# Local attention's scores in pairs of 32-row products, with one query mask for each batch

## What is computed

```
q, k, v = h @ wq_loc + bq_loc, h @ wk_loc + bk_loc, h @ wv_loc + bv_loc   # 16 heads of 8 features
for each query i, head h:                      # window: keys i-32 .. i+32
    s[j]  = q[i,h] . k[j,h] / sqrt(8) + rel_bias[j - i + 64]
    p     = softmax over the keys j of the window inside the sequence
    out   = sum_j p[j] v[j,h]
```

## Time and profile before

| what | value |
|---|---|
| time, median of 3 runs | 2551.7 us (2546.4 to 2554.1) |
| time of the profiled execution | 2552.2 us |
| its span, first to last instruction | 2550.4 us |
| TensorE busy | 2287.9 us, 90% |
| VectorE, ScalarE, GpSimd busy | 62%, 55%, 37% |
| mean granted clock | 0.959 |
| one loop body (seven of them) | 304.2 to 307.6 us |
| body "first" ends, body "second" begins | 225.7, 2372.9 us |

### The profile page before, as it was taken

How to read it: one execution, slowest core, us unless ns; L and a number is a source line. 1 busy time by engine, 2 the same in 40 slices (tenths; PEclk the granted TensorE clock), 3 DMA queues, 4 the chain that set the end, 5 groups by cost and what they waited for, 6 DMA issues and landing times. The chain is left out here.

```text
span 2550.4 us, 44510 instructions
## 1 busy us (share of the span) xinstructions
PE 2287.9 (90%) x16136; PEld 1618.0 (63%) x16136; DVE 1576.4 (62%) x4246; ACT 1398.1 (55%) x3824; POOL 946.1 (37%) x1058
## 2 busy tenths in 40 slices
PE   7668998989989899999999899898998989989897
PEld 5455666856668466675667656676666756658465
DVE  4555676566665666757666576656676566765752
ACT  4335563755547555566555565465563655647542
POOL 2333551245521544216433165132561235521540
PEclk9878999999999999999999999999999999999999
DMA  4000001000010000100001100000001000010001
GB/s 139 1 1 26 1 2 34 18 31 1 1 42 10 31 1 1 50 15 17 1 6 46 31 1 1 26 26 31 1 1 34 18 31 1 1 42 10 30 1 46
DMA packets 24877, 51.33 MB, mean 20 GB/s; under 512 B 3316, under 2 KB 3900, under 8 KB 24252
## 3 DMA queue, kind: packets, MB, share of 16 engines
q1 hardware_dynamic: 24636, 48.15, 5.8%
HBM read 46.04 MB, written 2.10 MB: 19 GB/s over the span
## 5 line engine op out<-in xcount | busy, mean ns | idle before, releaser
L857 POOL TENSOR_TENSOR rstd<-ve,half_neg 128x4 f32<-128x4 f32 (+1 forms) x56 | 66.4, 1190 | 861.8 <-DVE ve L840 861.8
L1313 PEld LDWEIGHTS ps<-wbuf,QK 128*128 128x128 f32 x2048 | 264.9, 192 | 107.5 <-issue 101.6
L1109 POOL TENSOR_TENSOR E<-E,ri 128x512 f32<-128x512 f32 x240 | 247.4, 1039 | 204.6 <-DVE ri L910 203.3
L1413 ACT ACTIVATE QK<-ps,cols 128x512 f32<-128x512 f32 x256 | 173.5, 686 | 215.1 <-PE ps L1292 214.5
L1292 PE MATMUL ps<-h2T,wbuf 128*128 128x512 f32 x512 | 279.3, 634 | 0.2
L1539 POOL TENSOR_TENSOR work<-work,ri 128x128 f32<-128x128 f32 x480 | 230.8, 505 | 128.4 <-DVE ri L1462 126.6
L748 ACT ACTIVATE E<-ps,nm 128x256 f32<-128x256 f32 x480 | 225.4, 485 | 85.2 <-DVE nm L903 84.4
L1313 PE MATMUL ps<-wbuf,QK 128*128 128x128 f32 x2048 | 267.9, 275 | 0.0
L1532 POOL TENSOR_TENSOR rn<-ss,half_neg 128x8 f32<-128x8 f32 x120 | 195.6, 1637 | 154.2 <-DVE ss L1438 153.5
L1376 ACT ACTIVATE work<-ps,nm 128x128 f32<-128x128 f32 x480 | 198.3, 426 | 81.0 <-DVE nm L1453 77.8
L903 DVE TENSOR_REDUCE nm<-ps 128x2 f32<-128x512 f32 x256 | 169.1, 683 | 98.0 <-PE ps L510 96.9
(11 more groups left out here) (278 smaller groups left out, 4806.3 us busy)
## 6 DMA issues: line engine op xcount, KB each, us to landing
wbuf<-in_w SPq DMA_DIRECT2D x128, 256.0 KB, 3.2
xT<-in_xT SPq DMA_DIRECT2D x9, 256.0 KB, 3.5
xr<-in_xr SPq DMA_DIRECT2D x9, 256.0 KB, 4.1
bias_t<-in_bias_t SPq DMA_DIRECT2D x1, 2048.0 KB
out_y<-xn SPq DMA_DIRECT2D x8, 256.0 KB, 2.0
wqkv<-in_wqkv SPq DMA_DIRECT2D x1, 1536.0 KB
wo<-in_wo SPq DMA_DIRECT2D x2, 512.0 KB, 8.9
rows<-in_rows SPq DMA_DIRECT2D x1, 531.0 KB, 7.2
```

Source lines behind the costliest of these rows:

```text
L1109: nc.gpsimd.tensor_tensor(L.E[:, g % 4, :, :], L.E[:, g % 4, :, :], L.ri[:, g, :].unsqueeze(2).broadcast_to((P, NT, S)), ALU.mult)\
L1313: last = nc.tensor.matmul(bank2[2 + x % 2][:, t * P:(t + 1) * P], hid[:, x % 2, c, t * P:(t + 1) * P], w2[:, x % WB, c, :], start=(c == 0) ...
L1413: nc.scalar.activation(hid[:, e % 2, f, :], bank2[u % 2], ACT.Gelu_apprx_tanh, bias=col("b1", e * FC + f)).then_inc(s["hid_ready"], 1)
```

## The change

Each head's eight features lie on eight partitions, so the 32 partitions 32g to 32g+31 hold the four heads of group g. The new kernel masks a query once for each position j of a head in its group (`rowmask`: for each partition, which of the four heads it belongs to), so one tensor of 1024 columns serves all four groups of a batch: one GpSimd instruction for each batch instead of four, both batches at once, in half of `GQ`. A score product then reads only the 32 partitions of its group. Two units with neighbouring groups are emitted together, instruction by instruction by turns, the one into bank 0 and the other into bank 1. `Sw` has four buffers instead of three, and the steps of TensorE, VectorE and ScalarE run through both batches without a break: units 0 to 15, the scores in eight pairs.

```diff
-        Qm = GQ[:, :, :].rearrange("p h (t q) -> p (h t q)", q=QT).rearrange("p (t h q) -> p t h q", t=4, q=QT)
+        Qm = GQ[:, 0:8, :].rearrange("p h n -> p (h n)").rearrange("p (b t j q) -> p b t j q", b=NP, t=4, q=QT)
...
+                nc.vector.tensor_reduce(rowmask[:, :], col("headmask", 0, WH).rearrange("p (g j) -> p j g", j=4), AX, ALU.add)
...
-                        pe.wait_ge(s["qm_ready"], 4 * b + g + 1)
-                        if U >= 2:
-                            pe.wait_ge(s["w_add"], U - 1)
-
-                        for n in range(4):
-                            h, t = 4 * g + n // 2 * 2, 2 * p + n % 2
-                            k = b * S + KEY0[t]
-                            last = nc.tensor.matmul(bank1[u % 2][:, n * P:(n + 1) * P],
-                                                    Qm[:, t, h:h + 2, :].rearrange("p h q -> p (h q)"), kloc[:, k:k + P],
-                                                    start=True, stop=True)
-                        last.then_inc(s["w_sc"], 1)
...
+            WU = 8 * NP
+            for v in range(WU // 2 + 2):
+                yield
+                if 2 * v < WU:
+                    b, u = divmod(2 * v, 8)
                     p, g = divmod(u, 4)
+                    pe.wait_ge(s["qm_ready"], b + 1)
+                    if v:
+                        pe.wait_ge(s["w_add"], 2 * v)
+                    for n in range(4):
+                        j, t = n // 2 * 2, 2 * p + n % 2
+                        k = b * S + KEY0[t]
+                        for i in range(2):
+                            r = 32 * (g + i)
+                            last = nc.tensor.matmul(bank1[i][:, n * P:(n + 1) * P],
+                                                    Qm[r:r + 32, b, t, j:j + 2, :].rearrange("p h q -> p (h q)"),
+                                                    kloc[r:r + 32, k:k + P], start=True, stop=True,
+                                                    skip_group_check=True)
+                            if n == 3:
+                                last.then_inc(s["w_sc"], 1)
...
+                if 0 <= 2 * v - 2 < WU:
+                    yield
+                    window_weights_T(2 * v - 2)
+                for V in (2 * v - 4, 2 * v - 3):
+                    if 0 <= V:
+                        yield
...
+                if 0 <= 2 * v - 1 < WU:
+                    yield
+                    window_weights_T(2 * v - 1)
...
+            for v in range(4 * NP + 1):
+                for i in range(2):
+                    yield
+                    if v:
+                        window_copy(2 * v - 2 + i)
+                    yield
+                    if v < 4 * NP:
+                        window_exp(2 * v + i)
...
-            def masked(b, g):
-
-                if b:
-                    pool.wait_ge(s["w_sc"], 8 * b - 4 + g + 1)
+            for b in range(NP):
                 shape = (P, 4, 4, QT)
-                nc.gpsimd.tensor_tensor(Qm[:, :, 4 * g:4 * g + 4, :],
+                nc.gpsimd.tensor_tensor(Qm[:, b, :, :, :],
```

More of the change, by code:

```diff
@@ new lines, in window_weights_T @@
+            def window_weights_T(V):
+                pe.wait_ge(s["w_exp"], V + 1)
+                if V:
+                    pe.wait_ge(s["w_et"], V)
+                else:
+                    pe.wait_ge(s["vm_ready"], NP)
+                for hd in range(4):
+                    last = nc.tensor.transpose(bank1[2][:, hd * P:(hd + 1) * P], Sw[:, V % 4, hd, :], ident[:, :])
+                last.then_inc(s["w_tr"], 1)
+            WU = 8 * NP
[3 more added lines that the diff above has]
+                    b, u = divmod(2 * v, 8)
+                    p, g = divmod(u, 4)
+                    pe.wait_ge(s["qm_ready"], b + 1)
[12 more added lines that the diff above has]
+                                last.then_inc(s["w_sc"], 1)
+                if v == 0:
+                    yield
+                    pe.wait_ge(s["lin_ready"], 1)
+                    transposed(bank1[2], lin).then_inc(s["lin_tr"], 1)
+                    yield
+                    pe.wait_ge(s["linT_ready"], 1)
+                    for a in range(NP):
+                        for t in range(4):
+                            k = a * S + KEY0[t]
+                            last = nc.tensor.matmul(bank1[3 - a][:, t * P:(t + 1) * P], hT[:, k:k + P],
+                                                    w1a[:, 5, :], start=True, stop=True)
+                        last.then_inc(s["vm_proj"], 1)
+                if 4 <= v and v % 4 == 2:
+                    yield
+                    window_T(v // 4 - 1)
+                if 0 <= 2 * v - 2 < WU:
[4 more added lines that the diff above has]
+                        yield
+                        b, u = divmod(V, 8)
+                        p, g = divmod(u, 4)
@@ L656, in first_pe @@
                         pe.wait_ge(s["w_et"], V + 1)
-                        if u == 3 and b:
+                        if u == 0 and b:
                             pe.wait_ge(s["winT_ready"], b)
@@ new lines, in first_dve @@
+                    dve.wait_ge(s["w_add"], V + 1)
+                    nc.vector.tensor_reduce(nmw[:, V % 4, :], Sw[:, V % 4, :, :], AX, ALU.max, negate=True)\
+                        .then_inc(s["w_max"], 1)
+                if v == 0:
+                    for a in range(NP):
+                        dve.wait_ge(s["vm_proj"], a + 1)
+                        nc.vector.tensor_copy(VW[:, a, :, :, 0:WD],
+                                              bank1[3 - a].rearrange("p (t h n) -> p t h n", t=4, h=WH))\
+                            .then_inc(s["vm_ready"], 1)
@@ L1075, in first_dve @@
+                if v and v % 4 == 1 and v >= 4:
+                    yield
+                    scaled(v // 4 - 1)
+            yield
             scaled(NP - 1)
```

175 lines of the change are left out of this document (62 added, 113 removed).

## The result

The changed kernel takes 2479.2 us (median of 4 runs, 2470.5 to 2480.8) against 2552.9 us for the kernel before in the same comparison: a ratio of 0.971, interval 0.968 to 0.974. Forecast was 2505, with 2487 to 2536 as the range; the kernel is faster than that range allows.

A forecast was written before the change was run, and what follows sets the result against it. TensorE's list of instructions was taken as the bound. Per loop body -7.1 + 0.6 + 1.0 = -5.5 us, 38.5 over seven, and 8 in body "first": 2551.7 - 38.5 - 8 = 2505 us, range 2487 to 2536.

The forecast's parts named there:

- Scores, -7.1 us: Local attention, loop body: paired score products overlap fully, so 16 groups of 0.89 us become 8; 14.2 us become 7.1.
- Changes of shape, 0.28 us a run: Local attention, loop body: each run of tiled instructions costs TensorE 0.28 us; two more runs add 0.6 us.
- ScalarE, +1.0 us: Local attention, loop body: pairs without other work go at ScalarE's 3.47 us; waits of 1.8 us against 0.8 before.
- no new stall and the old ones gone: Best end of the range for a loop body: -7.3 us, where the sum took -5.5.
- Rival (1): Local attention: ScalarE and VectorE take over, pairs without other work still cost 4.2 us; 2535 us, chance 0.14.
- GpSimd, 0: Loop body: eight masks of 2.02 us become two; they hide, worth 0, at most 2.0 us a body.
- Heads' order, 0 +- 10 us: Part before local attention: new order strings taken as 0, bounded by 1.5 us a body either way, 10 in all.
- End of the body, "stays as it is": End of the loop body: no change; the last division waits on VectorE behind the second half's layer norm.
- Body "first", -8 us: Local attention of body "first": steps run through both batches, ending at 200.5 instead of 208.5; 8 us, between 4 and 10.
- (3): Local attention: the pairs don't run side by side, scores still cost 14.2 us a body; 2551 us, chance 0.04.
- (4): Heads' parts: their new order costs its whole bound or more; 2515 to 2545 us, chance 0.10.
- (2): Local attention: TensorE's clock falls in pairs without other work, slower than before; 2581 us, chance 0.06.

The follow-up runs named there:

- the kernel with the parted value products: Changed kernel with the second unit's value products behind the pair's second transposes instead of beside the first unit's: 2545.4 us, ratio 0.998.
- the 128-row one: Changed kernel with score products that read all 128 partitions of queries and keys instead of 32: 2504.4 us, ratio 0.983.
- two of the experiments: Changed kernel with one unit's score products ahead of the other's (2619.3 us), and with second unit's value products behind the pair's second transposes (2545.4 us).
- A third: Changed kernel with two further GpSimd masks of the same size, read by nobody, behind the two real ones: 2508.7 us, ratio 0.984.

## Why the prediction fell short

- **The bound** was read right: TensorE's list of instructions sets the stretch, and what left the list was won. The sign, the mechanism and the place of the main term held.
- **Scores, -7.1 us:** right, or 0.8 us too much. Couples run side by side, fully if a change of shape costs 0.18 us and nearly so if it costs 0.13.
- **Changes of shape, 0.28 us a run:** borne out. A run has two changes, and one costs 0.13 us by the kernel with the parted value products and at most 0.18 by the 128-row one, so 0.27 to 0.36; for two more runs the difference is under 0.2 us.
- **ScalarE, +1.0 us: this step failed.** I took its pace from a stretch where TensorE delivered a unit each 2.10 us, so 1.74 us held small delays of the others; alone it does a unit in 1.65. Then a bare pair is TensorE's (3.35 us, against my 3.27 for it), and the waits that I had traced (1.8 us) came to 0.17. With this term turned round the stretch lies at the end that the text gave as "no new stall and the old ones gone", -7.3: the measured 71.55 to 64.21 is -7.3. That is 13 us over seven bodies. Rival (1) is out by the same rows.
- **GpSimd, 0: this step failed too, by about as much.** "They hide" looked at whether somebody waits for a mask, and not at what a mask does to an engine beside it. The cost was in the trace: instructions of 128x512 on VectorE take 0.69 us, and this one took 2.39, with GpSimd's masks beside it and TensorE waiting 2.25 us behind. TensorE's wait shrank by 1.75 us, over seven bodies 12 of the 21.5 us that the heads' parts gave. In the kernel before, taking the masks out of the way was worth 8 to 9 us of the time.
- **Heads' order, 0 +- 10 us:** the bound was fair. What is left of the heads' 21.5 us, some 9, can hold my 0.5 us a body for fewer changes of shape and the order's possible 6 us; it is not settled. The clock is not in it: its mean over these parts is 0.967 before and 0.966 after.
- **End of the body, "stays as it is":** wrong by 1 us a body the other way, +7.3 in all. TensorE's last product now ends 0.83 us ahead of VectorE's last instruction in the pass shown, 0.49 before; the rest of the longer gap (7.09 against 5.57 us, both with no releaser) is between the bodies. It is 5.2 to 6.2 us on average in the other variants of the changed kernel too, and no run here tells why.
- **Body "first", -8 us:** 5.7. The clock was 0.50 from 159.3 to 172.9 us, over the first pairs; before it had risen by 164.6. With the masks out of the way it was at full speed there (0.50 only from 191.6 on) and the stretch took 35.5 us, 8.2 less than 43.66. So the run-through was priced about right, and what the clock does at its start was not in the sum.
- **Rivals:** (3) is refuted by the 128-row kernel. (4) did not come, the heads' parts got shorter. (2) did not come either, but was nearer than its 0.06 says: two of the experiments lost the clock in the bare pairs. A third, which changes no product on TensorE, lost it ahead of the first score, which is not rival (2)'s mechanism.

Together: -46.5 forecast, -13 for the stalls, -21.5 for the heads, +7.3 for the gap, +2.3 for "first", -2.4 after the loop, makes -73.8 against 73.6.

## What to carry to other kernels

Before pricing work on GpSimd at nothing, look for VectorE instructions of one shape whose duration differs from place to place, and see what GpSimd does beside the long ones; who waits for the mask is only half of its cost. An engine's pace is to be taken from a stretch where nothing else holds it back. Where a stretch of small products holds the full clock, its margin is worth a trial with a wait or two added: here 2.8 us of added cost in a pass brought up to 12 us more from the clock.

## What the runs showed of the hardware

- Sixteen instructions over 32 partitions with 128 columns (float32): 1.64 us one unit's after the other's, 1.09 in couples on neighbouring groups into two banks, both with the changes of shape; 1.79 over 128 partitions.
- A change of tile shape costs TensorE 0.13 us (ten more of them: 52.45 against 51.11 us busy) to 0.18 us (sixteen, if couples overlap fully).
- One unit's after the other's, the 32-row products brought the granted clock down to 0.50 for 30 to 38 us of a stretch in which TensorE was never idle; by turns over 128 partitions, and in couples in the changed kernel, it stayed at 1.00. In couples with ten more changes of shape and 1.4 us of waits it fell in six of seven passes.
- A VectorE product of two inputs in SBUF, 128x512: 0.69 us alone, 1.4 to 2.4 us beside GpSimd's products, which themselves go from 1.91 to 2.36 us.
